# Perceiver layer on one core: four of seventeen double tiles of the attention's value product in three fp32r passes

## What is computed

```python
hidden_states = jnp.concatenate([context, latents], axis=1)      # 4096 + 256 rows
q = (latents @ Wq).reshape(b, q_len, 4, 8, 128)                  # 32 heads, 4 key/value heads
k = (hidden_states @ Wk).reshape(b, kv_len, 4, 128)
v = (hidden_states @ Wv).reshape(b, kv_len, 4, 128)
scores = jnp.einsum('bqhgd,bkhd->bhgqk', q, k) * scale
attn = jax.nn.softmax(scores, axis=-1)
out = jnp.einsum('bhgqk,bkhd->bqhgd', attn, v)
return out.reshape(b, q_len, 4096) @ Wo
```

## Time and profile before

| | us |
|---|---|
| median of 3 runs | 2001.52 |
| lowest, highest | 2000.62, 2008.04 |
| the profiled execution | 1999.74 |
| its span in the profile | 1997.9 |
| stage 1 | 0 to 382 |
| cross attention | 382 to 1371 |
| output projection | 1371 to 1466 |
| linear attention and the rest | 1466 to 1998 |

### The profile page before, as it was taken

The page is one execution under the profiler, slowest core; times in us unless marked ns, Lnnn a source line. Parts: engine busy times, 40 slices in busy tenths (PEclk is TensorE's granted clock), DMA queues, the critical chain, the costliest instruction groups (busy, mean ns, idle before and its releaser), DMA issues. The chain is left out here.

```text
span 1997.9 us, 26905 instructions
## 1 busy us (share of the span) xinstructions
PE 1960.9 (98%) x9725; PEld 1516.6 (76%) x9725; DVE 1233.5 (62%) x1294; ACT 952.7 (48%) x1015; POOL 839.3 (42%) x410
## 2 busy tenths in 40 slices
PE   9999999999999999999999999998999999999998
PEld 7888888866666666666666666545899999999876
DVE  4432221266777777877677877787756666666556
ACT  3211110155665565665665665654635444555442
POOL 2545441026776666766767766783000000000200
PEclk9999999999999999999999999999999999999999
DMA  8788875420032210321112210014735544445462
GB/s 306 301 305 318 327 271 190 173 99 25 24 111 90 72 49 15 111 97 56 49 52 92 79 61 1 6 58 180 282 138 189 185 177 175 178 182 189 139 232 99
DMA packets 72224, 283.85 MB, mean 142 GB/s; under 512 B 6400, under 2 KB 24320, under 8 KB 56512
## 3 DMA queue, kind: packets, MB, share of 16 engines
q1 hardware_dynamic: 65216, 232.31, 32.3%
q0 software_dynamic: 6912, 50.33, 6.6%
HBM read 212.89 MB, written 69.73 MB: 141 GB/s over the span
## 5 line engine op out<-in xcount | busy, mean ns | idle before, releaser
L705 POOL TENSOR_TENSOR xa_sums<-xa_sums,stage 128x1024 f32<-128x1024 f32 x150 | 362.7, 2418 | 39.3 <-ACT stage L649 33.1
L903 PE MATMUL xa_o_ps<-stage,xa_v 128*128 128x512 f32 x768 | 361.8, 594 | 4.5 <-ACT stage L649 4.5
L769 DVE TENSOR_TENSOR xa_peak<-xa_s_ps,xa_peak 128x1024 f32<-128x1024 f32 x224 | 273.0, 1219 | 71.4 <-PE xa_s_ps L115 70.8
L113 PE MATMUL xa_s_ps<-xa_qT_hi,split 128*128 128x512 f32 x544 | 304.7, 560 | 6.2 <-issue 3.5
L631 ACT ACTIVATE xa_rows<-xa_s_ps 128x1024 f32<-128x1024 f32 x208 | 213.6, 1027 | 102.0 <-DVE xa_peak L769 69.9
L790 DVE TENSOR_TENSOR xa_rows<-xa_rows,xa_r_ps 128x1024 f32<-128x1024 f32 x208 | 248.1, 1195 | 0.0
L903 PEld LDWEIGHTS xa_o_ps<-stage,xa_v 128*128 128x128 f32 x768 | 144.2, 190 | 116.9 <-issue 99.2
L705 POOL TENSOR_TENSOR xa_sums<-xa_sums,xa_probs 128x1024 f32<-128x1024 f32 x75 | 178.9, 2386 | 124.7 <-ACT xa_probs L649 122.1
L115 PE MATMUL xa_s_ps<-xa_qT_hi,split 128*128 128x512 f32 x544 | 214.4, 394 | 0.0
L114 PE MATMUL xa_s_ps<-xa_qT_lo,split 128*128 128x512 f32 x544 | 212.6, 391 | 0.0
L649 ACT ACTIVATE stage<-xa_rows 128x1024 f32<-128x1024 f32 x144 | 152.5, 1060 | 66.5 <-DVE xa_rows L790 61.6
(11 more groups left out here) (308 smaller groups left out, 4629.7 us busy)
## 6 DMA issues: line engine op xcount, KB each, us to landing
pair_raw<-in_w_qk SPq DMA_DIRECT2D x15, 2048.0 KB, 7.7
pair_raw<-in_w_gv SPq DMA_DIRECT2D x15, 2048.0 KB, 7.7
kv_w_raw<-in_wq POOLq DMA_DIRECT2D x16, 1024.0 KB, 8.3
wq_hi_scratch<-x_hT_hi POOLq DMA_DIRECT2D x16, 1024.0 KB, 4.5
wq_lo_scratch<-x_hT_lo POOLq DMA_DIRECT2D x16, 1024.0 KB, 5.3
full<-in_wo SPq DMA_DIRECT2D x16, 1024.0 KB, 5.1
pair_raw<-in_w_out SPq DMA_DIRECT2D x16, 1024.0 KB, 5.0
xa_w_hi<-wq_hi_scratch SPq DMA_DIRECT2D x15, 1024.0 KB, 4.8
```

Of the source, the lines that this page charges most:

```text
L113: pe.matmul(out, w_hi, m_hi, start=first, stop=False)
L705: pool.tensor_tensor(sums[:, :, :], sums[:, :, :], probs[j % KEEP], ALU.add).then_inc(added, 1)
L769: dve.tensor_tensor(peak[:, :, :], s_ps[:, 2 * b:2 * b + 2, :], peak[:, :, :], ALU.max).then_inc(peak_done, 1)
L903: last = pe.matmul(o_ps[:, :], v[:, at], probs[j % KEEP][:, t, :], start=j == 0 and t == 0, stop=j == J - 1 and t == 1)
```

## The change

In the slot of every pair, four of the 17 double tiles (j = 2, 6, 10, 14; SPLIT_STEPS) have their value product in three fp32r passes. For that:

- Stage 1: the values of these double tiles are rounded on the copy out of PSUM, and VectorE subtracts to get their low parts, in three pieces (split_values), in every second chunk. SP stores them (store_low). They are read out of free corners of other buffers.
- The loads of values (load_values) become runs of plain and split tiles: 16 DMAs for a group in place of 4.
- ScalarE writes the exponential of such a tile twice: in fp32, for the sums, and in fp32r (probs_hi). GpSimd subtracts the one from the other (pool_low, into probs_lo), right behind its addition of that j. TensorE waits for GpSimd's subtraction in these steps. Both buffers are single.
- The ring of probability buffers has four in place of three (KEEP), and shifts and exponentials run two double tiles ahead in place of one (AHEAD).
- To make room, x leaves SBUF during the cross attention and is loaded a second time in the output projection, between the third and the fourth half load; the reciprocals share a buffer with the sum row; the rounded identity and ones are made in the first block and are the only ones.

```diff
@@ stage 1
+        def split_values(dve, c, t, i):
+            dve.wait_ge(v_ready, VT * c + t + 1)
+            dve.tensor_copy(v_out[:, :, t, :].bitcast(F32R), v_ps[:, t, :].rearrange("p (g d) -> p g d", d=D)).then_inc(v_rounded, 1)
+            dve.wait_ge(v_rounded, 2 * i + t + 1)
+            if t == 0 :
+                dve.wait_ge(shared.low_stored, 16 * LOWS * i)
+            for which, g0, g1, tile in low_pieces:
+                if which == t:
+                    last = dve.tensor_tensor(tile, v_ps[:, t, g0 * D:g1 * D].rearrange("p (g d) -> p g d", d=D),
+                                             v_out[:, g0:g1, t, :], ALU.subtract).then_inc(low_copied, 1)
+            dve.wait_ge(low_copied, LOWS * i + (1 if t == 0 else LOWS))
+            dve.sem_inc(v_copied, 1)
@@ stage 2
-KEEP = 3
+SPLIT_STEPS = (2, 6, 10, 14)
+SPLIT = len(SPLIT_STEPS)
+KEEP = 4
+AHEAD = 2
@@ def load_values(sp, g, i):
-            at = piece_columns(i)
-            sp.dma_start(v[:, at], v_dram[bass.ds(g, 1)].rearrange("g p t d -> (g p) (t d)")[:, at]).then_inc(v_in[i], 16)
+            source = v_dram[bass.ds(g, 1)].rearrange("g p t d -> (g p) (t d)")
+            for j0, j1 in value_runs(i):
+                to = f32(v_hi[:, split_columns(j0)]) if j0 in SPLIT_STEPS else v[:, plain_columns(j0, j1)]
+                sp.dma_start(to, source[:, 2 * P * j0:2 * P * j1]).then_inc(v_in[i], 16)
+                if j0 in SPLIT_STEPS:
+                    low = low_dram[bass.ds(g, 1)].rearrange("g p t d -> (g p) (t d)")
+                    sp.dma_start(f32(v_lo[:, split_columns(j0)]), low[:, split_columns(j0)]).then_inc(v_in[i], 16)
@@ def act_exp(act, n, j, first=False, last=False):
             act.activation(probs[j % KEEP], rows[j], ACT.Exp, scale=SCALE).then_inc(exp_done, 1)
+            if j in SPLIT_STEPS:
+                i = SPLIT_STEPS.index(j)
+                if i > 0:
+                    act.wait_ge(pv_done, J * n + SPLIT_STEPS[i - 1] + 1)
+                elif not first:
+                    act.wait_ge(pv_done, J * (n - 1) + SPLIT_STEPS[-1] + 1)
+                act.activation(probs_hi[:, :, :], rows[j], ACT.Exp, scale=SCALE).then_inc(probs_hi_ready, 1)
@@ def act_slot(act, n, u, g, first=False, last=False):
-                if j + 1 < J:
-                    act_exp(act, n, j + 1, not has_prev, not has_next)
+                if j + AHEAD < J:
+                    act_exp(act, n, j + AHEAD, not has_prev, not has_next)
@@ GpSimd
+        def pool_low(pool, n, j):
+            pool.wait_ge(exp_done, J * n + j + 1)
+            pool.wait_ge(probs_hi_ready, SPLIT * n + SPLIT_STEPS.index(j) + 1)
+            pool.tensor_tensor(probs_lo[:, :, :], probs[j % KEEP], f32(probs_hi[:, :, :]), ALU.subtract).then_inc(low_by_pool, 1)
@@ def dve_slot(dve, n, u, g, first=False, last=False):
-                if j + 1 < J:
-                    dve_shift(dve, n, j + 1)
+                if j + AHEAD < J:
+                    dve_shift(dve, n, j + AHEAD)
@@ def pe_values(pe, n, j, values, first, last_slot):
+            if j in SPLIT_STEPS:
+                pe.wait_ge(low_by_pool, SPLIT * n + SPLIT_STEPS.index(j) + 1)
+                for t in range(2):
+                    at = slice(split_columns(j).start + t * P, split_columns(j).start + (t + 1) * P)
+                    last = three_pass(pe, o_ps[:, :], v_hi[:, at], v_lo[:, at], probs_hi[:, t, :], probs_lo[:, t, :],
+                                      False, False)
+                last.then_inc(pv_done, 1)
+                return
@@ first block
+                pool.wait_ge(zero_done, 3)
+                pool.tensor_copy(ident_r[:, :], eye)
+                pool.tensor_copy(ones_r[:, :], one)
@@ output projection
         def load_first_pair(sp, i):
+            if i == 3:
+                sp.dma_start(x_sb[:, :, :], x).then_inc(x_in, 16)
             weights.load_half(sp, i // 2, i % 2)
```

More of the change, by code:

```diff
@@ L282, in _ @@
             sp.dma_start(x_sb[:, :, :], x).then_inc(x_in, 16)
-            with sp.Fori(0, NCHUNK - 3) as c:
-                sp.wait_ge(c_lo_ready, c + 1)
-                load(sp, c + 2)
-                store(sp, c, VT)
+            sp.wait_ge(c_lo_ready, 1)
+            load(sp, 2)
+            store(sp, 0, VT)
+            with sp.Fori(0, (NCHUNK - 4) // 2) as i:
+                for par in range(2):
+                    c = 2 * i + 1 + par
+                    sp.wait_ge(c_lo_ready, c + 1)
+                    load(sp, c + 2)
+                    store(sp, c, VT)
+                    if par == 0:
+                        store_low(sp, c, i)
             sp.wait_ge(c_lo_ready, NCHUNK - 2)
@@ L478, in starts_piece, with plain_columns, split_columns, value_runs @@
     return j == 0 or j in ENDS
-def cross_attention(nc, wq_drams, k_drams, v_dram, hT_hi, hT_lo, ident, ones, oT_dram, shared, proj, last_pair):
+def plain_columns(j0, j1):
+    back = sum(s < j0 for s in SPLIT_STEPS)
+    return slice(2 * P * (j0 - back), 2 * P * (j1 - back))
+def split_columns(j):
+    i = SPLIT_STEPS.index(j)
+    return slice(2 * P * i, 2 * P * (i + 1))
+def value_runs(i):
+    runs, start = [], ENDS[i - 1] if i else 0
+    for j in range(start, ENDS[i]):
+        if j in SPLIT_STEPS:
+            if start < j:
+                runs.append((start, j))
+            runs.append((j, j + 1))
+            start = j + 1
+    if start < ENDS[i]:
+        runs.append((start, ENDS[i]))
+    return runs
+def cross_attention(nc, wq_drams, k_drams, v_dram, low_dram, hT_hi, hT_lo, ident, ident_r, ones_r, oT_dram, shared, proj, last_pair):
     with ExitStack() as ctx:
@@ L677, in act_slot @@
                 act_output(act, n, not has_prev)
-                act_exp(act, n + 1, 0)
+                for j in range(AHEAD):
+                    act_exp(act, n + 1, j, last=last and u == 2)
         @block.scalar
@@ L839, in _ @@
             dve_max(dve, 0, True)
-            dve_shift(dve, 0, 0)
+            for j in range(AHEAD):
+                dve_shift(dve, 0, j)
             slots(dve, dve_slot)
@@ L921, in pe_sums_last @@
             for i, part in enumerate(pieces):
-                last = pe.matmul(t_ps[:, :], ones[:, :], part, start=i == 0, stop=i == len(pieces) - 1)
+                last = pe.matmul(t_ps[:, :], f32(ones_r[:, :]), part, start=i == 0, stop=i == len(pieces) - 1)
             last.then_inc(sum_spread, 1)
```

103 lines of the change are left out of this document (71 added, 32 removed).

## The result

| | before | after |
|---|---|---|
| median (lowest to highest) | 2001.52 (2000.62 to 2008.04), 5 runs | 2016.79 (2014.35 to 2019.95), 5 runs |
| the profiled execution, its span | 1999.74, 1997.9 | 2016.96, 2015.0 |

The ratio of the runs is 1.0068, with a 95% interval of 1.0053 to 1.0082: slower, by 11 to 16 us. The forecast was 2010, its range 1993 to 2020.

A forecast was written before the change was run, and what follows sets the result against it. TensorE was taken to bound the kernel, busy 1960.9 of 1997.9 us. The terms -1.4 - 3.3 + 2.5 + 9.3 + 0.8 + 0.5 = +8.4 gave 2008.1 on the profiled execution, 2009.9 on the median, given as 2010; range 1993 to 2020.

The forecast's parts named there:

- a pair keeps a part, the last pair pays: Whole kernel: pairs 1 to 13 keep -0.25 us each of -1.42, the last pair costs +9.3; chance 0.63, range 2004 to 2015.
- The saving: Split steps on TensorE: six fp32r matmuls replace two fp32 ones, saving 0.35 us a step, 1.42 a pair.
- Rival C: Split steps: fp32r passes into a bank shared with fp32 matmuls cost as much as fp32; over 2200 us; chance 0.02.
- GpSimd in time in the pairs: Steady pairs: GpSimd's fourth low part is ready at 539.7, 0.5 us before TensorE's step 14 at 540.2.
- Rival B: Every pair: GpSimd becomes the bound, 1.2 us a pair, 16 in 13 pairs, 2026 us in all; chance 0.13.
- The order on ScalarE: Steps 7 and 8: row copies behind second exponentials cost TensorE 0.1 and 1.1 us; pairs 1 to 13 give -3.3.
- Rival A: Pairs 1 to 13 keep their whole saving, -18.5 us for -3.3; total -6.8, 1994.7 us; chance 0.22.
- Pair 14: No query projection before it, so GpSimd has no lead and TensorE waits for the fourth low part: +2.5 us.
- The last pair: No next pair's scores hide GpSimd's work; TensorE waits for low parts: +9.3 us, ends +6.5 and +12.
- Start: First block: two rounding copies and a wait delay the first load: +0.8 us, 0.3 to 1.2.
- x again: Output projection: one more 1 MB load of x, 2.6 us of transfer mostly covered: +0.5 us, ends 0 and 2.6.
- At nothing: Stage 1's subtractions, SP's extra stores and the sixteen value loads cost nothing; uncovered, the loads would cost 5 us once.

The follow-up runs named there:

- e11_no_vector_adds: The changed kernel with three of VectorE's four probability-block additions (8, 12, 16) left out of the last pair's sums; 2012.04 us in its one run.
- e1_row_first: The changed kernel with ScalarE's second exponential issued behind the row copy of the same round instead of ahead; 2016.01 us, ratio to before 1.0034 to 1.0064.

## Why the prediction held, and which of its steps didn't

The time lay inside the range, and my forecast of what happens, "a pair keeps a part, the last pair pays", is what happened. The time is 6.8 above the 2010, and 1.8 above the 2015 at which the forecast's own range ended. By the medians of the first table the change costs 15.3 us, by before's later medians (2003.44 with after's first runs, 2002.75 with its later ones) 13.4 and 11.9, for the 8.4 predicted. The pairs kept more than forecast, and the last pair and x cost more; that these misses have opposite signs is luck.

1. **The saving** of 0.35 a step, 1.42 a pair: right. Split steps that nothing holds up take 2.75 for 3.10, and pair 0, with no reciprocals, gave -1.36 and -1.39 for -1.4. Rival C fell.
2. **GpSimd in time in the pairs**: right, and closer than I said: 539.7 was forecast and 541.66 came, because it starves twice, 1.03 and 0.98 before additions 9 and 10. It was still 0.13 ahead of TensorE. Rival B was 0.13 us a pair away, and it showed at once when the row copy was moved.
3. **The order on ScalarE**: right in place and kind, wrong in size. Steps 7 and 8 lose 0.13 and 0.80 for the forecast 0.1 and 1.1: the two exponentials follow each other at 0.96 for the 1.06 that I took, and row 8, ready at 525.09, was wanted at 524.44 (522.72 and 1.72). A pair kept 0.49, not 0.25. Rival A didn't come, and no single edit brings it: the row copy, GpSimd and VectorE's round follow each other within 0.5 us.
4. **Pair 14**: the number was right (+3.0 for +2.5), its reason half right. The fourth low part is ready 46.3 us after GpSimd's first addition, for the 46.2 forecast, but in both traces of after TensorE comes 0.4 later still, 2.07 late for row 0 and with lower clock behind it, and so finds it ready. The step that failed is that I took GpSimd's lack of a lead into account and not ScalarE's: without the query projection, row 0 has no cover either. Where the clock stays up (e11_no_vector_adds) or row 0 comes earlier (e1_row_first), the wait of my forecast appears (1.42 and 1.48), and the pair is as long. That both limits come out alike is luck.
5. **The last pair**: the mechanism was right, four waits for GpSimd; the low part was ready 41.7 after the first addition, for 41.2. The term was too small by what comes behind it: three steps at a forecast 4.8 took 6.56, because the clock is at its lower level after the wait. +11.6 and +11.5 for +9.3, within its ends. Of the four "vector additions" one is a copy with a single input (0.98 long); beside it, too, GpSimd took 2.80 for 2.38.
6. **Start**: the first load is issued 0.59 later (2.69 for 2.10), +0.8 was forecast. The rest is the clock's: with half of the half-clock time taken off, the first addition of pair 0 is at 434.5, 433.6 and 434.4 in before and at 434.6 and 435.3 in after.
7. **x again**: the term that failed most, +0.5 with an end at 2.6, against 1.8 and 4.4. I counted the transfer (2.6 us) as mostly covered, and took the cover from one step of before. It isn't there: the waits alone are the 1.8 of the first trace and the 4.1 of e11_no_vector_adds, both at clock 1.00. In the second trace 1.7 of the 4.4 is the clock behind the wait, which I hadn't counted either.
8. **At nothing**: nothing of it shows in the marks. The stretch up to GpSimd's first addition, stage 1 and all its stores, moved by less (+1.85, -0.84) than after's two traces differ (2.8), and the slots in which values are loaded are as long as the others (pair 3 takes 59.41, pairs 7 and 11 59.38).

What was left out altogether: the steady part of before has no lower clock, and so I priced waits at their length. Behind several waits of 2 us and more came stretches at the lower level. What they cost depends on what TensorE waits for next: 1.7 us behind the last wait of the last pair and 1.7 in the second trace's projection, but nothing that shows in pair 14 or between the last pair's other waits, where GpSimd's next low part was the later of the two. With the executions' own differences in the start and in the unchanged code left aside, the kernel's terms add up to 0.6 - 1.4 - 5.4 (the mean of -6.4 and -4.4) + 3.0 + 11.5 + 1.8 to 4.4 = 10.1 to 12.7 us, near the 11.9 to 13.4 of the medians.

## What to carry to other kernels

Where work is moved to engines with a few tenths of slack, write down the whole order of the next two or three limits: here three of them lay within 0.5 us of a pair, single repairs gave 0.23 and -0.5, and two together gave 0.45 of the 0.93 that was missing. Look at the first and last pass of a software pipeline by themselves, since what hides the new work in the middle isn't there; four changed tiles cost 11.5 us in the last pair and saved 6 to 8 in the first 14, and leaving that pair as it was took the loss away (2001.41 beside before's 2003.34). And don't explain a difference of 0.3% between two profiled executions before a second trace of each is at hand.

## What the runs showed of the hardware that I had not expected

- A wait of TensorE can be followed by a stretch at half clock: behind waits of 2.07, 2.11, 3.96 and 4.39 us the windows had 0.86, 0.79, 0.83 and 0.88, with fp32 steps of 2.90 for 1.88. It isn't so each time. Behind the same 2.07, and behind 2.31, e11_no_vector_adds had 1.00; behind the 2.56 ahead of the last pair before takes 5.24 for eight matmul records and after 3.67. Behind waits of 1.31 and 1.50 the windows had 1.00.
- VectorE's and GpSimd's operations on 128x1024 fp32 with all inputs in SBUF went one behind the other. The one that started first took its usual 1.2 or 2.4 us; the other ended 1.1 us (VectorE's) or 2.2 us (GpSimd's) after it. So one subtraction of VectorE's took anything from 1.22 to 3.35, by when it started. With one input in PSUM VectorE's took 1.21, and GpSimd's beside it 2.38.
- Unchanged code of 531 us took 530.8 to 537.4 us in 14 executions of eleven kernels, with 7 to 21 us of it at half clock; half of that taken off leaves 525.8 to 528.9.
